# Attention kernel: the even transposes' bank is emptied between the exponentials of a pair's two heads

## The chip, the core and the metric

The kernel runs on one core of one Trainium2 chip. The metric is device time in microseconds (us) of one execution; the median of three runs of the kernel before is 1466.72 us (1466.05 to 1467.21). The engines are TensorE (PE in the rows, its weight loads PEld), VectorE (DVE), ScalarE (ACT), GpSimd (POOL) and SyncE (SP), which issues the loads and stores. Each engine works through its own queue in order, and they keep step by semaphores.

## What is computed

Sixteen blocks (batches) of 256 tokens by 256 features go through a first block of projections, then an attention with 16 heads of 64, then a layer of 8 experts. The change touches the attention alone. Of its reference:

```
shift = jax.nn.silu(t) @ W_ada.T + b_ada
h = _ln(x, ln1_g, ln1_b) + shift
qkv = (h @ Wqkv.T).reshape(b, n, 3, H, HD)
q = _ln(qkv[:, :, 0].transpose(0, 2, 1, 3), qn_g, qn_b)
k = _ln(qkv[:, :, 1].transpose(0, 2, 1, 3), kn_g, kn_b)
v = qkv[:, :, 2].transpose(0, 2, 1, 3)
scores = jnp.einsum('bhnd,bhmd->bhnm', q, k) / jnp.sqrt(jnp.float32(HD))
attn = jax.nn.softmax(scores, axis=-1)
o = jnp.einsum('bhnm,bhmd->bhnd', attn, v)
o = o.transpose(0, 2, 1, 3).reshape(b, n, H * HD)
x = x + o @ Wout.T
```

All matrix products but the values' and the transposes are made of three products of high and low parts.

## The kernel before

The attention runs over blocks t (written out one after the other, -2 to 17, of which 0 to 15 exist), and in each over pairs s = 0 to 7 of two heads, called the first and the second head (side 0 and 1). While block t's scores run, block t + 1's q, k and v are made ready, and the layer norm of block t + 2. Every engine has a function step(t, odd) in which the order of its queue is written by hand.

TensorE in pair s: the scores of both heads (scores, line 1103, into banks 3 and 4, one for each head); the transposes of the previous pair's probabilities (line 1115, banks 5 and 6); the fill of slot 2s, which I call the even one (four transposes into bank 0, called tr); the chunks of products for q, k, v of the next block (line 147, banks 1 and 2); in pairs 2 and 3 the output projection; the fill of slot 2s + 1, the odd one, again into bank 0; and in every second pair the value products of two pairs (line 1130). A table names what stands in the slots: x2 in slot 1, the layer norm's h in 2 (line 1192), the gates' products in 3 (line 1206), and eight transposes of q and k in slots 5 and 7 to 13 (line 1196). The even slots in use are thus 2, 8, 10 and 12: pairs 1, 4, 5 and 6. Before a fill, tr_free waits until ScalarE has emptied bank 0 of the one before:

```
TR_FILLS = [("x2", 0, 1), ("h", 0, 2), ("gates", 0, 3), ("qk", 0, 5)] + [("qk", j, 6 + j) for j in range(1, 8)]
```

ScalarE in pair s: the odd bank of the pair before (empty, line 1282 for q and k, with the norm's scale and bias); the values' high part (o_h, line 1328); two exponentials for each head (exps, line 1258), which wait for the row minima that VectorE takes of the scores (shift, line 1483); the copy of the transposed probabilities out of bank 5 (pT, line 1340); the high parts of q and k that are due (high_parts, line 1315); the even bank (empty; in pair 1 line 1276); and the copies of the chunks (lines 1302, 1304, 1309). VectorE takes the reciprocals of the sums (share_p, line 1489), GpSimd multiplies the probabilities with them (line 1382), and only then may TensorE transpose them in the next pair. GpSimd also scales q and k (line 1370) and makes low parts (lines 1376, 1408); the one of line 1408, rowsT_l, waits for VectorE's cast of line 1537 and is needed by the first chunk of pair 6. In block 14 the last fill of q and k is moved from slot 13 to 14 (LAST_NEAR, LATE_FILL), and block 15 has no next block to prepare.

Of the kernel before, what the change touches and what calls it, by code (L numbers as in the profile page):

```python
# [40 lines left out]
def live(b):  # L41

    return not isinstance(b, int) or 0 <= b < NB
# [824 lines left out]
PAIRS = H // 2  # L868
# [25 lines left out]
LAST_NEAR = NB - 2, 6  # L894
# [37 lines left out]
def attention(nc, exponent, weights, rows_of, banks, ident, x1_rows, hbias, cols, x2_rows, logit, out, a, halves, sbuf, sems):  # L932
# [4 lines left out]
    s = ExitStack()  # L937
    with s:
# [29 lines left out]
        def first(b):  # L968

            return isinstance(b, int) and b == 0  # L970
# [77 lines left out]
        with nc.Block() as block:  # L1048
# [200 lines left out]

            @block.scalar  # L1250
            def _(act):
                def exps(t, s):
                    for side in range(2):
                        at = s % 2 * 2 + side
                        wait(act, lowest, H, t, 2 * s + side + 1)
                        wait(act, pT_done, H, t, 2 * s + side - 3)
                        for n in range(TT):
                            last = nc.scalar.activation(prob[at][:, n, :], score_bank[side][:, n * T:(n + 1) * T], ACT.Exp,  # L1258
                                                        bias=shift[:, at, n:n + 1], scale=-1.0, accum_out=denom[:, at, n:n + 1])
                        last.then_inc(exped, 1)  # L1260

                def seeds(b, n):
                    wait(act, rooted, 2 * TT, b, 2 * n + 1)
                    nc.scalar.activation(logs[:, :], ssq[:, n, :], ACT.Ln).then_inc(seeded, 1)
                    wait(act, seeded, 2 * TT, b, 2 * n + 1)
                    wait(act, normed, 8, b - 1, (n + 1) * QKC)
                    nc.scalar.activation(rq[:, n, :], logs[:, :], ACT.Exp, scale=-0.5).then_inc(seeded, 1)

                def empty(b, name, j, its):
                    if name is None or not live(b) or name == "h" and first(b):  # L1270
                        return
                    if name == "h":
                        wait(act, tr_h, 1, b, 1)
                        wait(act, a_lo, 1, b - 1, 1)
                        for k in range(KT):
                            last = nc.scalar.activation(aT[:, k, :], tr[:, k * T:(k + 1) * T], ACT.Identity,
                                                        bias=hbias[:, k, bass.ds(b, 1)], scale=cols[:, LN1_G + k:LN1_G + k + 1])
                        last.then_inc(out_h, 1)
                    if name == "qk":
                        wait(act, tr_qk, 8, b, j + 1)  # L1280
                        g = QN_G if QK_ORDER[j] % QKC < 2 else KN_G
                        nc.scalar.activation(raw_block(j), tr[:, :].rearrange("p (m n) -> p m n", m=4), ACT.Identity,  # L1282
                                             bias=cols[:, g + 1:g + 2], scale=cols[:, g:g + 1]).then_inc(out_qk, 1)
                    if name == "x2":
                        wait(act, tr_x2, 1, b, 1)
                        nc.scalar.activation(x2T[:, :, :].rearrange("p k n -> p (k n)"), fill_bank(b)[:, :], ACT.Copy).then_inc(out_x2, 1)
                    if name == "gates":
                        wait(act, tr_gates, 1, b, 1)
                        nc.scalar.activation(logit[:, bass.ds(b * TT, TT), :], fill_bank(b)[:, 0:TT * E].rearrange("p (n e) -> p n e", n=TT), ACT.Copy).then_inc(out_gates, 1)

                def projected(b, n):
                    wait(act, tr_proj, TT, b, n + 1)
                    wait(act, tr_gates, 1, b - 1, 1)
                    nc.scalar.activation(proj[:, n, :], proj_bank(b, n)[:, 0:D], ACT.Copy).then_inc(out_proj, 1)

                def chunk(b, j, odd):
                    n, c = CHUNKS[j]
                    wait(act, chunk_done, 12, b, j + 1)
                    if c < QKC:
                        e = n * QKC + c  # L1300
                        wait(act, qk_lo, 8, b - 1, QK_ORDER.index(e) + 1)
                        nc.scalar.activation(raw[:, e, :], chunk_bank[j % 2][:, :], ACT.Copy)  # L1302
                        wait(act, summed, 8, b, e - 1)
                        nc.scalar.activation(raw_sq[e % 2][:, :], chunk_bank[j % 2][:, :], ACT.Square).then_inc(chunk_out, 1)  # L1304
                    else:
                        wait(act, pv_done, PAIRS, b - 2, PAIRS)
                        if isinstance(b, int) and b == 1:
                            act.wait_ge(wo_lo, FIRST_LO + 4)
                        nc.scalar.activation(v[1 - odd][:, n, (c - QKC) * 512:(c - QKC + 1) * 512], chunk_bank[j % 2][:, :], ACT.Copy).then_inc(chunk_out, 1)

                def high_parts(t, s, js, odd):
                    for j in js:
                        if live(t + 1) and HIGH_PAIR[j] == s:
                            wait(act, out_qk, 8, t + 1, j + 1)
                            nc.scalar.activation(block_of((qT_h, kT_h), j, 1 - odd), raw_block(j), ACT.Copy).then_inc(qk_hi, 1)

                def step(t, odd):
                    for s in range(PAIRS):
                        if not closing(t) and not closing(t - 1):
                            if s - 1 in PROJ_PAIRS and live(t - 1):  # L1320
                                projected(t - 1, PROJ_PAIRS.index(s - 1))
                            empty(*fill_at(t, 2 * s - 1), 1 - odd)
                        for b, q, its, n in taken_at(t, s, odd):
                            if live(b):
                                wait(act, pv_done, PAIRS, b, q + n)
                                if q in (0, 2):
                                    wait(act, tr_proj, TT, b - (2 if q == 0 else 1), TT)
                                nc.scalar.activation(o_part(o_h, q, its, n), result_of(b, q, n), ACT.Copy).then_inc(o_hi, n)
                        if closing(t) or closing(t - 1):
                            empty(*fill_at(t, 2 * s - 1), 1 - odd)  # L1330
                        for n in range(TT):
                            if live(t + 1) and s == SEED_PAIR[n]:
                                seeds(t + 1, n)
                        if live(t):
                            exps(t, s)
                        b, q, _ = pair_at(t, s, 1, odd)
                        if live(b):
                            wait(act, pT_done, H, b, 2 * q + 1)
                            wait(act, pv_done, PAIRS, b, q - 1)
                            nc.scalar.activation(pT[q % 2 * 2][:, :, :].rearrange("p m n -> p (m n)"), pT_bank[0][:, :], ACT.Copy).then_inc(pT_act, 1)  # L1340
                        late = t == LAST_NEAR[0] and s == PAIRS - 1
                        high_parts(t, s, range(7 if late else 8), odd)
                        empty(*fill_at(t, 2 * s), 1 - odd)
                        if late:
                            high_parts(t, s, (7,), odd)
                        for c, j in chunks_at(t, s):
                            if live(c):
                                chunk(c, j, odd)
                        if closing(t) and s in PROJ_PAIRS:
                            projected(t - 1, PROJ_PAIRS.index(s))  # L1350
                        for q in range(4):
                            if t == -1 and s == WOUT_HIGH_PAIR[q]:
                                nc.scalar.activation(flat(wo_h[:, :, :])[:, q * 512:(q + 1) * 512], flat(o_raw)[:, q * 512:(q + 1) * 512], ACT.Copy).then_inc(wo_hi, 1)
                        if live(t) and s == PIECE_PAIRS[0]:
                            wait(act, ew_piece, 32, t, 16)
                            wait(act, ew_stored, 32, t - 1, 32)
                            nc.scalar.activation(ew_h[:, :], ew_raw[:, :], ACT.Copy).then_inc(ew_piece, 8)
                steps(step)

            @block.gpsimd  # L1360
# [768 lines left out]
```

## Time and profile before

| | us |
|---|---|
| median of three runs | 1466.72 |
| lowest, highest | 1466.05, 1467.21 |
| the profiled execution | 1464.1 |
| its span | 1462.3 |
| TensorE busy (weight loads) | 1376.4 (1178.4) |
| ScalarE busy | 1038.9 |
| VectorE busy | 960.8 |
| GpSimd busy | 913.1 |

The attention's blocks stand between about 365 and 1190 us of the span. In a row of the timeline stand the start, the duration, the engine, the line, the operation, what it writes from what, and, where the engine was idle before it, how long and for whom. Ends of matrix products are modelled, so that the starts are the safer times. Where a row merges several instructions (x4), the duration is that of all.

### The profile page before, as it was taken

How to read it: one execution, taken by the hardware profiler on the slowest of the kernel's cores; microseconds unless marked ns; L12 is line 12 of the kernel's file. 1: busy time of each engine (PE TensorE's matmuls, PEld its weight loads, DVE VectorE, ACT ScalarE, POOL GpSimd, SP SyncE). 2: the span in 40 equal slices, each digit the busy share in tenths (PEclk: the TensorE clock that was granted, in tenths of full speed). 3: DMA queues.
4: the chain of work that ended last, by engine and by line, in shares of the span. 5: the costliest groups of instructions: out<-in, count | busy, mean ns of one | idle time of the engine just before them, and what ended most of it. 6: DMA issues, size and time to landing. Idle time of an engine off the chain costs nothing. (4 is left out here: it accounts for less than half of the span.)

```text
span 1462.3 us, 30429 instructions
## 1 busy us (share of the span) xinstructions
PE 1376.4 (94%) x10795; PEld 1178.4 (81%) x10795; DVE 960.8 (66%) x2191; ACT 1038.9 (71%) x2703; POOL 913.1 (62%) x855
## 2 busy tenths in 40 slices
PE   7899999998899999999999999999999889899997
PEld 5799999996677787787787777787778678889896
DVE  5877767645666566567666667667656568678763
ACT  5566666547888888888888888878888742466662
POOL 2676676543767867776776776876786730364633
PEclk9899999999999999999999999999999999999999
DMA  5432222110100110110110010010011028144622
GB/s 156 132 106 73 66 68 72 48 38 21 37 29 9 51 44 9 52 44 9 51 52 22 31 51 23 31 51 33 20 44 38 23 71 332 35 111 122 168 34 29
DMA packets 61638, 89.04 MB, mean 61 GB/s; under 512 B 6144, under 2 KB 50992, under 8 KB 58800
## 3 DMA queue, kind: packets, MB, share of 16 engines
q1 hardware_dynamic: 53232, 75.82, 16.0%
q0 software_dynamic: 6144, 8.39, 3.5%
q10 hardware_dynamic: 2112, 2.88, 0.6%
q8 instruction: 87, 1.43, 0.4%
q14 instruction: 63, 0.52, 0.1%
HBM read 61.90 MB, written 25.18 MB: 60 GB/s over the span
## 5 line engine op out<-in xcount | busy, mean ns | idle before, releaser
L1382 POOL TENSOR_TENSOR prob<-prob,share_p 128x512 f32<-128x512 f32 x256 | 271.5, 1067 | 229.3 <-DVE share_p L1489 228.7
L1483 DVE TENSOR_REDUCE shift<-bank 128x2 f32<-128x512 f32 x256 | 164.6, 684 | 251.3 <-PE bank L1103 251.1
L1258 ACT ACTIVATE prob<-bank,shift 128x256 f32<-128x256 f32 x512 | 235.7, 474 | 87.0 <-DVE shift L1483 86.9
L147 PE MATMUL bank<-wqkv_h,rowsT_h 128*128 128x512 f32 x384 | 159.0, 414 | 2.8 <-PEq L311 1.7
L147 PE MATMUL bank<-wqkv_h,rowsT_l 128*128 128x512 f32 x384 | 150.9, 393 | 0.0
L147 PE MATMUL bank<-wqkv_l,rowsT_h 128*128 128x512 f32 x384 | 150.8, 393 | 0.0
L1115 PE MATMUL bank<-ident,prob 128*128 128x128 f32 x1024 | 142.5, 281 | 1.3 <-POOL prob L1382 1.3
L1370 POOL TENSOR_TENSOR landing<-landing,rq 128x512 f32<-128x512 f32 x128 | 132.0, 1052 | 8.4 <-DVE rq L1437 8.4
L1130 PE MATMUL bank<-pT,landing 128*64 128x256 f32 x1024 | 126.2, 386 | 1.2 <-ACT pT L1340 1.2
L1115 PEld LDWEIGHTS bank<-ident,prob 128*128 128x128 f32 x1024 | 109.3, 141 | 21.7 <-POOL prob L1382 4.2
L1196 PE MATMUL bank<-ident,landing 128*128 128x128 f32 x512 | 79.2, 278 | 34.4 <-ACT landing L1282 31.9
L640 POOL TENSOR_TENSOR hid_l<-hid,hid_h 128x512 fp32r<-128x512 f32 x64 | 86.2, 1356 | 30.7 <-ACT hid_h L536 30.0
L1258 ACT ACTIVATION_READ_ACCUMULATOR prob<-bank,shift 128x1 f32 x512 | 104.7, 205 | 0.0
L1282 ACT ACTIVATE landing<-bank,cols 128x512 f32<-128x512 f32 x128 | 102.9, 804 | 2.2 <-PE bank L1196 0.6
L532 ACT ACTIVATE hid<-bank,cols 128x256 f32<-128x256 f32 x128 | 53.3, 470 | 68.2 <-PE bank L147 68.2
L1196 PEld LDWEIGHTS bank<-ident,landing 128*128 128x128 f32 x512 | 58.1, 142 | 53.5 <-issue 47.5
L1130 PEld LDWEIGHTS bank<-pT,landing 128*64 128x64 f32 x1024 | 67.2, 136 | 40.4 <-issue 9.3
L1103 PE MATMUL bank<-kT_h,qT_h 64*128 64x256 f32 x512 | 85.7, 330 | 3.1 <-ACT prob L1258 3.1
L1302 ACT ACTIVATE landing<-bank 128x512 f32<-128x512 f32 x128 | 80.4, 628 | 10.2 <-PE bank L147 10.2
L1514 DVE COPY pT<-bank 128x512 f32<-128x512 f32 x128 | 87.1, 680 | 0.2 <-PE bank L1115 0.2
L1479 DVE TENSOR_REDUCE ssq<-raw_sq 128x8 f32<-128x512 f32 x128 | 85.8, 672 | 1.3 <-ACT raw_sq L1304 0.7
L147 PEld LDWEIGHTS bank<-wqkv_h,rowsT_h 128*128 128x128 f32 x384 | 72.8, 190 | 16.3 <-issue 2.4
(324 smaller groups left out, 4528.2 us busy)
## 6 DMA issues: line engine op xcount, KB each, us to landing
landing<-in_fc1s SPq DMA_DIRECT2D x6, 1024.0 KB, 4.9
landing<-in_fc2s SPq DMA_DIRECT2D x6, 1024.0 KB, 5.0
rows<-in_x SPq DMA_DIRECT2D x16, 256.0 KB, 3.0
xT<-in_xT SPq DMA_DIRECT2D x16, 256.0 KB, 2.7
x_again<-in_x SPq DMA_DIRECT2D x16, 256.0 KB, 2.7
x_rows<-x SPq DMA_DIRECT2D x16, 256.0 KB, 3.2
rows<-x_rows SPq DMA_DIRECT2D x16, 256.0 KB, 3.1
x<-x_rows SPq DMA_DIRECT2D x16, 256.0 KB, 2.8
```

Source lines behind the costliest of these rows:

```text
L147: last = nc.tensor.matmul(out, a, b, start=(n == 0), stop=(n == 3 * len(ks) - 1))
L640: nc.gpsimd.tensor_tensor(hid_l[:, 2 * g:2 * g + 2, :], hid[:, 2 * g:2 * g + 2, :], hid_h[:, 2 * g:2 * g + 2, :].bitcast(F32), ALU.subtrac ...
L1115: last = nc.tensor.transpose(pT_bank[side][:, m * T + n * P:m * T + (n + 1) * P], prob[q % 2 * 2 + side][:, n, m * P:(m + 1) * P], ident[: ...
L1130: last = nc.tensor.matmul(values_bank(b, q)[side * HD:(side + 1) * HD, :], v[its][:, m, h * HD:(h + 1) * HD], pT[q % 2 * 2 + side][:, m, : ...
L1196: last = nc.tensor.transpose(tr[:, m * P:(m + 1) * P], raw_block(j)[:, m, :], ident[:, :])
L1258: last = nc.scalar.activation(prob[at][:, n, :], score_bank[side][:, n * T:(n + 1) * T], ACT.Exp, bias=shift[:, at, n:n + 1], scale=-1.0, ...
L1282: nc.scalar.activation(raw_block(j), tr[:, :].rearrange("p (m n) -> p m n", m=4), ACT.Identity, bias=cols[:, g + 1:g + 2], scale=cols[:, g ...
L1370: nc.gpsimd.tensor_tensor(part, part, rq[:, n, c * 8:(c + 1) * 8].unsqueeze(2).to_broadcast([P, 8, HD]), ALU.mult).then_inc(normed, 1)
L1382: nc.gpsimd.tensor_tensor(prob[at][:, :, :], prob[at][:, :, :], share[:, at, :].unsqueeze(2).to_broadcast([P, TT, T]), ALU.mult).then_inc( ...
L1479: nc.vector.tensor_reduce(ssq[:, n, c * 8:(c + 1) * 8], raw_sq[c % 2][:, :].rearrange("p (h d) -> p h d", h=8), AX, ALU.add).then_inc(summ ...
L1483: nc.vector.tensor_reduce(shift[:, s % 2 * 2 + side, :], score_bank[side][:, :].rearrange("p (n m) -> p n m", n=TT), AX, ALU.min).then_inc ...
L1514: nc.vector.tensor_copy(pT[q % 2 * 2 + 1][:, :, :].rearrange("p m n -> p (m n)"), pT_bank[1][:, :]).then_inc(pT_dve, 1)
```

## The change

ScalarE's step is written in another order. exps gets a list of sides, and is called once for the first head and once for the second; between the two calls stands the emptying of the even bank, which before came behind the copy of pT and the high parts. In pair 7 of block 14 (late) it stays where it was. No other engine's code is touched, and no instruction is added or left out.

```
-                def exps(t, s):
-                    for side in range(2):
+                def exps(t, s, sides):
+                    for side in sides:
...
+                        late = t == LAST_NEAR[0] and s == PAIRS - 1
                         if live(t):
-                            exps(t, s)
+                            exps(t, s, (0,))
+                        if not late:
+                            empty(*fill_at(t, 2 * s), 1 - odd)
+                        if live(t):
+                            exps(t, s, (1,))
...
-                        late = t == LAST_NEAR[0] and s == PAIRS - 1
                         high_parts(t, s, range(7 if late else 8), odd)
-                        empty(*fill_at(t, 2 * s), 1 - odd)
                         if late:
+                            empty(*fill_at(t, 2 * s), 1 - odd)
                             high_parts(t, s, (7,), odd)
```

ScalarE's queue in pairs 5 and 6 of a block, before (L1282 is written once for the even bank, once for the odd one; L1258 x4 are the exponentials of both heads):

```order
L1328 ACTIVATE o_h<-bank 128x512
L1258 ACTIVATE prob,denom<-bank,shift 128x256 x4
L1340 ACTIVATE pT<-bank 128x512
L1315 ACTIVATE kT_h<-landing 128x4x128 x2
L1282 ACTIVATE landing<-bank,cols 128x512
L1309 ACTIVATE landing<-bank 128x512 x2
L1282 ACTIVATE landing<-bank,cols 128x512
L1258 ACTIVATE prob,denom<-bank,shift 128x256 x4
L1340 ACTIVATE pT<-bank 128x512
L1315 ACTIVATE qT_h<-landing 128x4x128
L1315 ACTIVATE kT_h<-landing 128x4x128
L1282 ACTIVATE landing<-bank,cols 128x512
```

And now (line 1340 has become 1345):

```order
L1328 ACTIVATE o_h<-bank 128x512
L1258 ACTIVATE prob,denom<-bank,shift 128x256 x2
L1282 ACTIVATE landing<-bank,cols 128x512
L1258 ACTIVATE prob,denom<-bank,shift 128x256 x2
L1345 ACTIVATE pT<-bank 128x512
L1315 ACTIVATE kT_h<-landing 128x4x128 x2
L1309 ACTIVATE landing<-bank 128x512 x2
L1282 ACTIVATE landing<-bank,cols 128x512
L1258 ACTIVATE prob,denom<-bank,shift 128x256 x2
L1282 ACTIVATE landing<-bank,cols 128x512
L1258 ACTIVATE prob,denom<-bank,shift 128x256 x2
L1345 ACTIVATE pT<-bank 128x512
```

The even bank's L1282 has moved ahead of two exponentials, the copy of pT and the high parts; the odd bank's stands where it stood.

ScalarE's queue in pair 1 of a block, before, where the even bank holds the layer norm's transposes (L1276):

```order
L1267 ACTIVATE rq<-logs 128x32
L1258 ACTIVATE prob,denom<-bank,shift 128x256 x4
L1340 ACTIVATE pT<-bank 128x512
L1276 ACTIVATE rowsT<-bank,hbias,cols 128x256 x2
L1302 ACTIVATE landing<-bank 128x512
```

And now:

```order
L1267 ACTIVATE rq<-logs 128x32
L1258 ACTIVATE prob,denom<-bank,shift 128x256 x2
L1276 ACTIVATE rowsT<-bank,hbias,cols 128x256 x2
L1258 ACTIVATE prob,denom<-bank,shift 128x256 x2
L1345 ACTIVATE pT<-bank 128x512
L1302 ACTIVATE landing<-bank 128x512
```

Both instructions of L1276 have moved ahead of the second head's exponentials and the copy of pT.

## Rows read from the trace of the kernel before

**Rows 1.** Attention: stretch, its us, busy us of PE PEld DVE ACT POOL, clock, DMA.
```profile
365.00:1190.00 825.00, 790.48 (x6087) 632.38 (x6087) 529.38 (x1170) 686.84 (x1917) 594.56 (x553) 1.00 0.11 34
```

**Rows 2.** Line 1196, what its engine sat idle for: us, times.
```profile
  ACT landing L1282: 31.9, 46
```

**Rows 3.** TensorE, pair 5 of block 6: start, us, engine, line, operation.
```profile
709.97 0.39 PE L1103 MATMUL bank<-kT_h,qT_h 64*128 64x256 f32 x2
...
711.81 0.60 PE L1196 MATMUL bank<-ident,landing 128*128 128x128 f32 x4
...
714.75 0.39 PE L147 MATMUL bank<-wqkv_h,rowsT_l 128*128 128x512 f32 x1
715.98 0.63 PE L1196 MATMUL bank<-ident,landing 128*128 128x128 f32 x4 [0.83 <-ACT landing L1282]
716.53 0.38 PE L1103 MATMUL bank<-kT_h,qT_h 64*128 64x256 f32 x2
```

**Rows 4.** ScalarE, pairs 5 to 7 of block 6, in order of time.
```profile
711.71 0.47 ACT L1258 ACTIVATE prob<-bank,shift 128x256 f32<-128x256 f32 x1 [0.97 <-DVE shift L1483]
...
713.52 0.61 ACT L1340 ACTIVATE pT<-bank 128x512 f32<-128x512 f32 x1
...
715.04 0.80 ACT L1282 ACTIVATE landing<-bank,cols 128x512 f32<-128x512 f32 x1
715.70 1.11 ACT L1309 ACTIVATE landing<-bank 128x512 f32<-128x512 f32 x2
716.65 0.82 ACT L1282 ACTIVATE landing<-bank,cols 128x512 f32<-128x512 f32 x1
718.27 0.48 ACT L1258 ACTIVATE prob<-bank,shift 128x256 f32<-128x256 f32 x1 [0.80 <-DVE shift L1483]
...
724.17 0.84 ACT L1282 ACTIVATE landing<-bank,cols 128x512 f32<-128x512 f32 x1
...
726.71 0.47 ACT L1258 ACTIVATE prob<-bank,shift 128x256 f32<-128x256 f32 x1 [0.96 <-DVE shift L1483]
```

**Rows 5.** TensorE, pair 4 of block 0: odd transposes that do not wait.
```profile
389.17 0.40 PE L147 MATMUL bank<-wqkv_h,rowsT_l 128*128 128x512 f32 x1
389.40 0.60 PE L1196 MATMUL bank<-ident,landing 128*128 128x128 f32 x4
```

**Rows 6.** TensorE, pairs 4, 6 and 1 (the block after).
```profile
706.83 0.39 PE L147 MATMUL bank<-wqkv_h,rowsT_l 128*128 128x512 f32 x1
707.53 0.63 PE L1196 MATMUL bank<-ident,landing 128*128 128x128 f32 x4 [0.32 <-ACT landing L1282]
...
721.37 0.39 PE L147 MATMUL bank<-wqkv_h,rowsT_l 128*128 128x512 f32 x1
722.54 0.63 PE L1196 MATMUL bank<-ident,landing 128*128 128x128 f32 x4 [0.79 <-ACT landing L1282]
723.10 1.95 PE L1130 MATMUL bank<-pT,landing 128*64 128x256 f32 x16
...
741.59 0.39 PE L147 MATMUL bank<-wqkv_h,rowsT_l 128*128 128x512 f32 x1
742.01 1.03 PE L1206 MATMUL bank<-wgate,proj 128*128 128x8 f32 x8
```

**Rows 7.** ScalarE, pair 1: the even bank with the layer norm.
```profile
740.83 1.04 ACT L1276 ACTIVATE rowsT<-bank,hbias,cols 128x256 f32<-128x256 f32 x2
```

**Rows 8.** VectorE, GpSimd and TensorE's weight loads, pairs 5 and 6.
```profile
714.23 0.17 DVE L1489 RECIPROCAL share_p<-denom 128x2 f32<-128x2 f32 x1
...
715.94 1.28 POOL L1408 TENSOR_TENSOR rowsT_l<-rowsT,rowsT_h 128x512 fp32r<-128x512 f32 x1 [0.43 <-DVE rowsT_h L1537]
...
718.70 0.19 PEld L147 LDWEIGHTS bank<-wqkv_h,rowsT_h 128*128 128x128 f32 x1
```

**Rows 9.** Block 14, pair 6: ScalarE's copy of pT, TensorE's values.
```profile
1145.65 0.61 ACT L1340 ACTIVATE pT<-bank 128x512 f32<-128x512 f32 x1
...
1146.31 1.08 PE L1130 MATMUL bank<-pT,landing 128*64 128x256 f32 x8 [0.76 <-ACT pT L1340]
```

## The prediction, made before the changed kernel was run

> **What bounds the kernel now.** I read the views in this order: busy time by stretch, what TensorE's groups wait for, then the timelines of TensorE and ScalarE through one block of the attention. The 16 blocks of the attention take 825 us of the 1462.3 us span and are nearly alike. In them [rows 1] TensorE is busy for 790.48 us, ScalarE for 686.84, GpSimd for 594.56, VectorE for 529.38, at a granted clock of 1.00. So TensorE sets the time, and what can be won is its idle time. The groups' view says where most of that is: the transposes of line 1196 sat idle 31.9 us in 46 waits for ScalarE's line 1282 [rows 2]. TensorE writes four transposes into bank 0, ScalarE copies the bank out with scale and bias, and TensorE may not write the next four before that.
>
> Counted along TensorE's timeline, three of the 46 lie in each of blocks 1 to 13 (pairs 4, 5, 6), two each in blocks 0 (pairs 5, 6) and 14 (pairs 4, 5), and three ahead of block 0, where ScalarE has no exponentials. It is always the odd transposes (the pair's second set) that wait for the bank of the even ones.
>
> Pair 5 of block 6 shows it. TensorE starts the scores at 709.97, the even transposes at 711.81 (over by 712.41), its last product of the pair at 714.75, and the odd transposes only at 715.98 [rows 3]. ScalarE does not empty the bank until 715.04 [rows 4]: ahead of it in its queue stand all four exponentials, the copy of pT and the two high parts of kT. The bank's contents have lain ready for 2.6 us by then. The wait is thus one of order, not of work.
>
> **What a stall costs.** Where nothing waits, the transposes start 0.23 us after the product before them (389.17 and 389.40) [rows 5]. In pair 5 they start 1.23 after it: 1.00 lost. Pair 6: 721.37 to 722.54, 1.17, so 0.94 lost. Pair 4: 706.83 to 707.53, 0.70, so 0.47 lost. The same thing happens in pair 1, where the even bank holds the layer norm's transposes (emptied by line 1276) and the gates' products follow: 741.59 to 742.01, 0.42, so 0.19 lost [rows 6]. Per block 2.60 us. The idle column says less (0.83 in pair 5 where I count 1.00), because it starts at the modelled end of the product before, which overlaps the next start. The Trainium skill warns of this (Perfetto Trace Analysis, Identifying the Most-Contended Engine): matmul busy time is a poor measure of headroom, since matmuls are pipelined. The trace agrees: 31.9 us of idle over 46 waits is 0.69 each, while starts against starts give 0.80 for the mean of pairs 4 to 6. By the idle column alone the 43 waits in the blocks would be worth 43 x 0.69 = 30 us instead of the sum below.
>
> **The change, part by part.** No instruction is added or removed. In pairs 1, 4, 5 and 6 ScalarE's emptying of the even bank moves ahead of the second head's two exponentials (block 14's pair 7 keeps the old order).
>
> (1) When does it now run? The four exponentials issue from 711.71 to 713.52 [rows 4], so the first head's two are through half-way, at 712.62: 2.65 after the scores' start. The even transposes are over at 2.44. So ScalarE does not wait for them, by 0.2 us. The emptying takes the slot from 2.65 and ends 0.80 later at 3.45; the odd transposes want the bank at 5.01 (714.75 + 0.23). They have 1.5 us to spare, and the whole stall goes. In pair 1 the two halves of line 1276 (1.04 us) [rows 7] end at 3.69, the gates want the bank at 5.0: it goes too.
>
> (2) What is later? The second head's exponentials, the copy of pT and the high parts, by the slot of the emptying: 715.70 - 715.04 = 0.66 us (0.90 in pair 1). From the slot in which the bank was emptied before, ScalarE's queue is as it was, since the same work stands ahead.
> - The copy of pT ended at 713.52 + 0.61, 4.16 after the scores; now 4.82. The value products that need it (pairs 4 and 6) start 0.56 after the odd transposes [rows 6], so now at 5.6: 0.8 to spare.
> - VectorE's reciprocal for the second head stood at 714.23 (4.26) because VectorE was late with other work; the exponentials are now over at 4.33, so it and the split of rowsT behind it slip by 0.10. GpSimd's low part of rowsT ran from 715.94 to 717.22, now 0.10 later; TensorE's first weight load that needs it stood at 718.70 and comes 1.00 sooner, at 717.70 [rows 8]. 0.4 us to spare, the narrowest place that I find.
> - The next pair's scores need the exponentials' end; in pair 5 they start at 5.56 instead of 6.56, against 4.33 for the exponentials.
>
> (3) Is ScalarE on time for the next pair? In pair 5 it starts its last piece, the odd emptying, at 716.65 and is free at 717.31; the exponentials of pair 6 stood at 718.27 after 0.80 of idle for the row minima [rows 4]. TensorE being 1.00 sooner, they are wanted at 717.27. ScalarE is 0.04 late, for the first time the one that is waited for, but the exponentials have 0.8 us in front of the next thing on TensorE. For pair 7 it starts the odd emptying at 724.17, which with the copy of the value products (o_h, 0.48) behind it keeps it until 724.17 + 0.66 + 0.48 = 725.31; the exponentials stood at 726.71 [rows 4] and are wanted 0.94 sooner, at 725.77, so 0.46 is left. From pair 7 on, each engine stands to TensorE as before. So the block runs 2.60 us shorter, with ScalarE 87% busy (686.84 of 825 less the 36 of the sum below) instead of 83.
>
> (4) Where it costs. In block 14's pair 6 TensorE has no chunk of products and no odd transposes; the values wait there for the copy of pT (0.76 idle, the copy starts at 1145.65) [rows 9]. The copy comes 0.66 later, and this time TensorE pays it.
>
> **Sum.** Pair 4: 14 blocks x 0.47 = 6.6. Pair 5: 15 x 1.00 = 15.0. Pair 6: 14 x 0.94 = 13.2. Pair 1: 12 (blocks 2 to 13, which have both layer norm and gates) x 0.19 = 2.3. Less 0.66 in block 14. Ahead of block 0 the emptying already waits for TensorE, and I take 0. Together 36.4 us. The profiled execution took 1464.1 us (span 1462.3), so 1427.7; the median of the runs is 1466.7, so **1430.3 us**.
>
> **Rivals.**
> (A) The stall goes, but a new wait takes a part. The candidates are the 0.4 us in front of GpSimd's low part and ScalarE's 0.04 us in pair 6, at 2.6 us less per block. For it: several margins shrink at once in pairs 5 to 7, and I replayed them from one block's durations. Against it: each of them is still positive, and after pair 7 there is slack again. If one pair per block gave back its 1.00 us, 14 us would be lost: 1444.
> (B) Nothing changes, because the odd transposes would next wait for GpSimd's normalised blocks (line 1370), which share their line with the bank's wait. Against it: the waits' view names ScalarE 46 times. 1466.7.
> (C) Slower. ScalarE now waits for a bank that TensorE fills only after the previous pair's transposes of prob, and these wait for GpSimd's division, which waits for the very exponentials that are put back. If the delay of the second head reached TensorE in all four pairs, as it does in block 14's pair 6, it would cost 3 x 0.66 + 0.90 = 2.88 a block against 2.60 won: 14 x 0.28 = 4 us more, 1471. It decides once the copy of pT or the division has under 0.66 us in hand; I find 0.8 after the delay at the copy, and more at the division.
> (D) The clock falls as TensorE has fewer gaps. Against it: it is 96% busy now and is granted 1.00 throughout [rows 1]. I give it nothing of its own.
>
> **Chances and range.** Forecast 0.78 (its own range 1426 to 1437, the far end by the idle column), A 0.14, B 0.03, C 0.05. A measurement of this kernel tells about 0.2% (3 us) from no change: faster 0.92, same 0.03, slower 0.05. Range 1426 to 1441: below, 4 us for stalls that I under-counted (each stalled set also runs 0.03 us longer) and blocks whose pair 6 lost a little more than block 6's; above, it takes in most of A.
>
> **What would show it.** In the profile after: line 1196's idle for line 1282 down from 31.9 us to the few of the prologue (under 5); the span from one block's scores to the next down by 2.6; exponentials in pair 6 starting about 0.04 us behind the minima; the wait of line 1130 for pT in block 14 at 1.4 instead of 0.76. Wrong would be: line 1282 idle for tens of us (the bank not full at 2.44), a wait of line 147 for rowsT_l in pair 6 (A), or line 1115 waiting for prob in steady blocks (C).

## The result, and the profile after

The changed kernel takes 1431.62 us (median of four runs, 1430.79 to 1432.67), the kernel before 1466.38 (four runs, 1464.22 to 1467.21). The ratio is 0.9766, with a 95% interval of 0.9749 to 0.9782: faster by 34.8 us. The forecast was 1430.3. The profiled execution took 1431.61 us, its span 1429.8.

The attention's blocks, by stretch (us, then busy us of PE, PEld, DVE, ACT, POOL, the granted clock, DMA share, GB/s); it answers to [rows 1]:

```profile
365.00:1160.00 795.00, 787.51 (x6115) 639.57 (x6113) 532.35 (x1175) 685.64 (x1920) 595.17 (x553) 1.00 0.11 36
```

TensorE's busy time has hardly moved (790.48 to 787.51), ScalarE's neither; a stretch that is 30 us shorter holds the same work. ScalarE is busy 685.64 of 795 us, 86%. The transposes of line 1196, and what their engine sat idle for (us, times); the row on line 1282 answers to [rows 2], 31.9 us in 46 waits:

```profile
  POOL landing L1374: 8.2, 7
  issue: 7.1, 17
  ACT landing L1282: 3.7, 3
```

The three waits left for line 1282 are those ahead of block 0. "issue" is idle time without a named releaser. The same view of the kernel before has under it

```profile
  issue: 47.5, 45
```

43 of these 45 stand at the weight loads of the very 43 odd sets whose matrix products waited for line 1282 (1.23 in pair 5, where 1.00 was lost), so it is the same loss, read in TensorE's other queue. The 17 that are left become important below.

TensorE through pair 5 of block 6, from its scores to the next pair's, and on through pair 6 (start, us, engine, line, operation):

```profile
695.62 0.39 PE L1103 MATMUL bank<-kT_h,qT_h 64*128 64x256 f32 x2
...
697.46 0.60 PE L1196 MATMUL bank<-ident,landing 128*128 128x128 f32 x4
...
700.40 0.40 PE L147 MATMUL bank<-wqkv_h,rowsT_l 128*128 128x512 f32 x1
700.64 0.60 PE L1196 MATMUL bank<-ident,landing 128*128 128x128 f32 x4
701.17 0.38 PE L1103 MATMUL bank<-kT_h,qT_h 64*128 64x256 f32 x2
...
703.27 0.63 PE L1196 MATMUL bank<-ident,landing 128*128 128x128 f32 x4
...
706.24 0.40 PE L147 MATMUL bank<-wqkv_h,rowsT_l 128*128 128x512 f32 x1
706.48 0.60 PE L1196 MATMUL bank<-ident,landing 128*128 128x128 f32 x4
```

The odd transposes start 0.24 after the last product (700.40 to 700.64), where it was 1.23 in [rows 3]; in pair 6 also 0.24 (706.24 to 706.48), where it was 1.17 in [rows 6]. Both stalls are gone. Something else is there too: in pair 5 the *even* transposes start 1.84 after the scores (697.46 - 695.62), in pair 6 2.10 after them (703.27 - 701.17). Their weight load stands in the queue PEld as

```profile
703.24 0.42 PEld L1196 LDWEIGHTS bank<-ident,landing 128*128 128x128 f32 x4 [0.31 <-issue]
```

so that it had waited 0.31 us, with no releaser named.

ScalarE beside it; these rows answer to [rows 4]:

```profile
698.27 0.78 ACT L1282 ACTIVATE landing<-bank,cols 128x512 f32<-128x512 f32 x1
698.93 0.48 ACT L1258 ACTIVATE prob<-bank,shift 128x256 f32<-128x256 f32 x1
...
699.83 0.61 ACT L1345 ACTIVATE pT<-bank 128x512 f32<-128x512 f32 x1
...
702.30 0.82 ACT L1282 ACTIVATE landing<-bank,cols 128x512 f32<-128x512 f32 x1
702.96 0.52 ACT L1258 ACTIVATE prob<-bank,shift 128x256 f32<-128x256 f32 x1
...
703.93 0.78 ACT L1282 ACTIVATE landing<-bank,cols 128x512 f32<-128x512 f32 x1
```

In pair 5 the even bank is emptied from 2.65 after the scores (698.27 - 695.62), as forecast, and its slot is 0.66 (to 698.93). The odd bank of pair 5 is emptied from 702.30, which is 1.13 after the scores of pair 6; before, it was 0.12 after them (716.65 to 716.53, [rows 3, 4]). ScalarE's queue stands where it stood, and TensorE has moved up by 1.00.

The length of each pair, from the start of its scores to the next scores, the same in blocks 2 to 13 within 0.04 us:

| pair | before | after | forecast of the difference | measured |
|---|---|---|---|---|
| 0, 2, 3, 7 together | 24.18 | 24.21 | 0 | +0.03 |
| 1 | 6.17 | 5.90 | -0.19 | -0.27 |
| 4 | 7.93 | 7.43 | -0.47 | -0.50 |
| 5 | 6.56 | 5.55 | -1.00 | -1.01 |
| 6 | 8.44 | 7.72 | -0.94 | -0.72 |
| the block | 53.28 | 50.80 | -2.60 | -2.48 |
| 6 of block 14 | 5.22 | 6.01 | +0.66 | +0.79 |

The span is 32.5 us shorter, and it adds up so: pair 4, 14 x 0.50 = 7.0; pair 5, 15 x 1.01 = 15.1; pair 6, 14 x 0.72 = 10.1; pair 1, 12 x 0.27 = 3.2; together 35.4. Against it: 0.8 in block 14's pair 6; 0.65 in block 15, whose pairs 0 and 1 now take 5.55 + 3.93 instead of 4.36 + 4.47; 0.4 ahead of block 0, which starts at 365.31 instead of 364.94 (364.3 to 366.3 in the traces below); and 1.0 behind the attention (from the scores of block 15's last pair to the end, 279.1 instead of 278.1). That last part runs the same instructions and differs from run to run (278.2 to 279.4 in the traces below), so I read nothing into either. The profiled execution of before lay 2.3 us under its median, which is why the medians differ by 34.8 and the spans by 32.5.

### The profile page after: what moved, and what is told of

It is laid out like the page before. It is cut to its first block and busy times, and to the rows that moved or that the text cites. A ratio compares the mean times of both kernels' runs of the same rounds, so it can differ in the third digit from the quotient of the medians.

```text
span 1429.8 us, 30429 instructions
## 1 busy us (share of the span) xinstructions
PE 1370.5 (96%) x10795; PEld 1183.3 (83%) x10795; DVE 960.7 (67%) x2191; ACT 1035.9 (72%) x2703; POOL 911.5 (64%) x855
## 5 line engine op out<-in xcount | busy, mean ns | idle before, releaser
L1258 ACT ACTIVATE prob<-bank,shift 128x256 f32<-128x256 f32 x512 | 237.8, 479 | 64.3 <-DVE shift L1487 64.2
L1258 ACT ACTIVATION_READ_ACCUMULATOR prob<-bank,shift 128x1 f32 x512 | 107.5, 210 | 0.0
L1282 ACT ACTIVATE landing<-bank,cols 128x512 f32<-128x512 f32 x128 | 101.9, 796 | 4.9 <-PE bank L1196 3.3
L147 PEld LDWEIGHTS bank<-wqkv_h,rowsT_l 128*128 128x128 f32 x384 | 72.5, 189 | 15.8
```

What stands on the lines that cost most here:

```text
L147: last = nc.tensor.matmul(out, a, b, start=(n == 0), stop=(n == 3 * len(ks) - 1))
```

## The experiments

The kernels below are compared in two ways. By time, each beside nine runs of the kernel before on the same chip (median 1466.15 for the first four, 1466.69 for the others). And by the lengths of the pairs in one profiled execution, which two profiled executions of the changed kernel give alike to 0.04 us in blocks 1 to 14; this tells differences of 0.1 us in a pair apart, which the times can't.

### Pair 5 alone

```
-                        if not late:
+                        moved = s == 5
+                        if moved:
                             empty(*fill_at(t, 2 * s), 1 - odd)
...
-                        if late:
+                        if not moved:
                             empty(*fill_at(t, 2 * s), 1 - odd)
+                        if late:
```

> Of the change only pair 5 is kept: the even bank is emptied between the two heads' exponentials there, and in the old place (behind the copy of pT and the high parts) in all other pairs. My theory: each pair's stall is a term of its own, so pair 5 is 5.55 us long as in the changed kernel instead of 6.56, and pairs 4 and 1 are as before (7.93, 6.17). Pair 6 keeps its old stall and is about 8.49, 0.05 more than before, since ScalarE reaches it 0.05 late; the new 0.26 us wait of the even transposes there hides in the old stall. 15 x 1.01 - 14 x 0.05 = 14.4 us less than before: about 1452. Rival (the won time is handed on to the next wait, ScalarE being the bound): pair 6 grows by most of what pair 5 wins, under 7 us won, 1460 or more.

Measured: 1450.18 us (1449.95 to 1451.93), ratio 0.9897 (0.9882 to 0.9912). Pair 5 takes 5.55, as in the full change; pairs 4 and 1 are as before (7.92, 6.17), and pair 6 is 0.10 *longer* than before, 8.54 against 8.44. TensorE in pair 6 of block 6:

```profile
709.21 0.39 PE L1103 MATMUL bank<-kT_h,qT_h 64*128 64x256 f32 x2
...
711.31 0.63 PE L1196 MATMUL bank<-ident,landing 128*128 128x128 f32 x4
...
715.32 0.63 PE L1196 MATMUL bank<-ident,landing 128*128 128x128 f32 x4 [0.65 <-ACT landing L1282]
```

The even transposes start 2.10 after the scores, as in the full change, though pair 6's own order is the old one. So it is the shorter pair 5 that makes them late, and not pair 6's own change. Here the odd set waits for ScalarE in any case, so the 0.26 us cost nothing; its wait is only shorter for them (0.65 instead of the 0.79 of [rows 6]). The 0.10 comes from ScalarE's emptying of the even bank, first in this version, then in the kernel before:

```profile
714.32 0.86 ACT L1282 ACTIVATE landing<-bank,cols 128x512 f32<-128x512 f32 x1
```

```profile
721.60 0.80 ACT L1282 ACTIVATE landing<-bank,cols 128x512 f32<-128x512 f32 x1
```

It starts 5.11 after the scores instead of 5.07 (709.21 and 716.53), since ScalarE reaches pair 6 late, and lasts 0.06 longer. The forecast had the first part and not the second.

### The odd bank of pair 5 emptied one instruction earlier

In the changed kernel's pair 5 the odd bank is full at 701.24 (700.64 + 0.60), and ScalarE starts the two copies of line 1309 at 701.34, with the emptying behind them. In this version the emptying stands between those two instead of behind both.

```
-                            empty(*fill_at(t, 2 * s - 1), 1 - odd)
+                            if s != 6:
+                                empty(*fill_at(t, 2 * s - 1), 1 - odd)
...
-                        for c, j in chunks_at(t, s):
+                        for n, (c, j) in enumerate(chunks_at(t, s)):
                             if live(c):
                                 chunk(c, j, odd)
+                            if n == 0 and s == 5:
+                                empty(*fill_at(t, 2 * s + 1), 1 - odd)
```

> The changed kernel, and besides ScalarE empties pair 5's odd bank between the copies of that pair's two chunks instead of behind them. Theory: what pair 6 won less than I forecast (8.44 to 7.72, where 7.47 was due) is a new wait of its even transposes, which start 2.10 us after the scores instead of 1.84 because the odd bank of pair 5 is not empty yet. ScalarE's emptying comes one copy (0.48 us) sooner, and this wait goes: pair 6 7.46 long, 14 x 0.26 = 3.6 us less than the changed kernel, 1428.0. Rival (the even transposes of pair 6 are late for another reason, or the second chunk's copy, now 0.66 later, holds TensorE up): pair 6 stays at 7.72, or its first or second chunk waits, 1431.6 or more.

Measured: 1427.98 us (1426.61 to 1430.92), ratio 0.9747 (0.9733 to 0.9760). Pair 6 takes 7.47 instead of 7.72; no other pair of a steady block differs. TensorE in pair 6 of block 6:

```profile
699.48 0.39 PE L1103 MATMUL bank<-kT_h,qT_h 64*128 64x256 f32 x2
...
701.31 0.60 PE L1196 MATMUL bank<-ident,landing 128*128 128x128 f32 x4
```

ScalarE at the same place:

```profile
699.65 0.62 ACT L1309 ACTIVATE landing<-bank 128x512 f32<-128x512 f32 x1
700.13 0.81 ACT L1282 ACTIVATE landing<-bank,cols 128x512 f32<-128x512 f32 x1
```

The emptying starts 0.65 after the scores instead of 1.13, and the even transposes are back at 1.83 after them. This shows the cause of the 0.25 us. It also shows where the view hid it: what line 1196's engine sat idle for now reads

```profile
  ACT landing L1282: 3.7, 3
  issue: 2.4, 2
```

Fifteen waits have left the row "issue" (17 to 2, and 7.1 to 2.4 us): 4.7 us, 0.31 each, as many as there are pairs 6 in blocks 0 to 14. They were waits for ScalarE that carried no name of a releaser, since they were seen at the weight load ahead of the transposes.

### Block 14 as before

```
-                        if not late:
+                        old = t == LAST_NEAR[0] and s >= PAIRS - 2
+                        if not old:
                             empty(*fill_at(t, 2 * s), 1 - odd)
...
-                        if late:
+                        if old:
                             empty(*fill_at(t, 2 * s), 1 - odd)
+                        if late:
```

> The changed kernel, but block 14's pair 6 keeps the old order (its pair 7 does already). Theory: the length of that pair falls from 6.01 to about 5.27 us, since the copy of pT, for which TensorE waits there, no longer stands behind the emptying: 0.7 us. The changed kernel's TensorE clock was granted at 0.5 (1.2 GHz) from 1118.9 to 1122.3 in block 15, right behind that longer wait (1.25 us idle) and another of 1.37; before the change, with 0.76 and 1.37, it was not. If the one brought the other, the lower clock goes too and block 15's pairs 0 and 1 together take 8.83 instead of 9.48: 1.4 us less than the changed kernel in all, 1430.2. Rival (the clock falls there by chance or by something else): it stays or comes and goes, 0.7 us less, 1430.9.

Measured: 1431.74 us (1430.13 to 1432.63), ratio 0.9765 (0.9751 to 0.9778). Pair 6 of block 14 falls from 6.01 to 5.33, by 0.68, the slot of the emptying. The 0.11 that stays over the 5.22 of before is ScalarE's, which TensorE waits for here: the exponentials start 1.79 after the scores instead of 1.74, and the copy of pT lasts 0.67 instead of the 0.61 of [rows 9]. The late odd bank of pair 5 has no part in it: the version with both remedies, below, empties that bank earlier, and this pair takes 5.34 there. TensorE's values in that pair, in the changed kernel; the second row answers to [rows 9], where it waited 0.76:

```profile
1109.82 1.08 PE L1130 MATMUL bank<-pT,landing 128*64 128x256 f32 x8
1112.15 1.08 PE L1130 MATMUL bank<-pT,landing 128*64 128x256 f32 x8 [1.25 <-ACT pT L1345]
```

The same in this version:

```profile
1111.97 1.08 PE L1130 MATMUL bank<-pT,landing 128*64 128x256 f32 x8
1113.63 1.08 PE L1130 MATMUL bank<-pT,landing 128*64 128x256 f32 x8 [0.57 <-ACT pT L1346]
```

The second question was block 15. In the changed kernel TensorE's granted clock there is low for a while, which it was not before. Busy time by stretch, over 6 us from block 15's start and over the low part of them, in the changed kernel (the granted clock is the third number from the right):

```profile
1117.00:1123.00 6.00, 5.78 (x40) 3.73 (x42) 3.77 (x11) 5.25 (x15) 5.59 (x6) 0.72 0.01 3
...
1119.00:1122.00 3.00, 3.00 (x14) 1.53 (x13) 1.84 (x5) 2.81 (x11) 3.00 (x3) 0.50 0.00 0
```

In this version, over the low part:

```profile
1121.00:1123.50 2.50, 2.50 (x12) 1.31 (x12) 1.33 (x4) 2.50 (x10) 2.50 (x3) 0.50 0.00 0
```

In the kernel before:

```profile
1151.00:1157.00 6.00, 5.32 (x48) 3.73 (x48) 4.44 (x12) 5.48 (x15) 5.59 (x6) 1.00 0.01 3
```

I had thought that the longer wait in block 14 brings the clock down. Here the wait is short again, and the clock falls all the same, to 0.50 of full speed (the 1.2 GHz level). That theory fell. In this trace there is a second such stretch in block 0's pair 4, which takes 9.91 us with it and 8.51 without:

```profile
387.00:390.00 3.00, 2.92 (x11) 2.73 (x12) 1.19 (x3) 1.70 (x6) 3.00 (x4) 0.50 1.02 338
```

So the 0.68 won in block 14 is not to be seen in the time, and it is less than two runs of one kernel differ by.

### Behind the copy of pT

```
-                        if not late:
-                            empty(*fill_at(t, 2 * s), 1 - odd)
                         if live(t):
                             exps(t, s, (1,))
...
+                        if not late:
+                            empty(*fill_at(t, 2 * s), 1 - odd)
                         high_parts(t, s, range(7 if late else 8), odd)
```

> The even bank is emptied right behind the copy of pT, ahead of the high parts, instead of between the two heads. Theory: the emptying only has to be over before the odd transposes want the bank, 5.01 us after the scores; there it ends at 4.83 in pairs 4 to 6, so these pairs are as in the changed kernel (7.43, 5.55, 7.72) within 0.05. In pair 1, which has no high parts, this is the old place: 6.17 again instead of 5.90, 3.2 us more. Block 14's pair 6 gets its 0.7 us back, and block 15 its clock: 1.4 less. In sum 1.8 us more than the changed kernel, 1433.4. Rival (the bank must be free early, or the delay of the second head's exponentials costs something everywhere): pairs 4 to 6 differ from the changed kernel by 0.1 us or more each, up if the first, down if the second.

Measured: 1432.73 us (1431.27 to 1434.99), ratio 0.9775 (0.9762 to 0.9789), so by time not to be told from the changed kernel. By pairs: pair 4 takes 7.42, pair 5 5.54, pair 6 7.77, and block 14's pair 6 5.35. The stalls of pairs 4 to 6 need the emptying ahead of the high parts only, not between the heads. Pair 1 takes 6.18, as before; there both instructions end too late for the gates' products. TensorE in this version:

```profile
675.40 0.39 PE L147 MATMUL bank<-wqkv_h,rowsT_l 128*128 128x512 f32 x1
675.84 1.03 PE L1206 MATMUL bank<-wgate,proj 128*128 128x8 f32 x8
676.80 0.38 PE L1103 MATMUL bank<-kT_h,qT_h 64*128 64x256 f32 x2
```

In the changed kernel:

```profile
674.73 0.40 PE L147 MATMUL bank<-wqkv_h,rowsT_l 128*128 128x512 f32 x1
674.96 0.95 PE L1206 MATMUL bank<-wgate,proj 128*128 128x8 f32 x8
675.85 0.39 PE L1103 MATMUL bank<-kT_h,qT_h 64*128 64x256 f32 x2
```

0.44 against 0.23 from the last product to the gates' products, and these last 0.96 against 0.89 to the next scores. So a set that had to wait also runs 0.07 longer, which is why pair 1 won 0.27 and not 0.19.

### How much delay the second head bears: pairs 4 and 5

The high parts of q and k, too, are put ahead of the second head's exponentials, one instruction of ScalarE in pair 4 (0.52 us more delay), two in pair 5 (1.04). In this version in pairs 4 and 5:

```
+                        ahead = s in (4, 5)
+                        if ahead:
+                            high_parts(t, s, range(8), odd)
                         if live(t):
                             exps(t, s, (1,))
...
-                        high_parts(t, s, range(7 if late else 8), odd)
+                        if not ahead:
+                            high_parts(t, s, range(7 if late else 8), odd)
```

> The changed kernel, and in pairs 4 and 5 ScalarE also makes the high parts of q and k (0.52 us in pair 4, two of them, 1.04 us, in pair 5) ahead of the second head's exponentials. It prices the margins of the forecast. Theory: in pair 4 the copy of pT ends 5.34 us after the scores, the values want it at 5.6, so pair 4 stays at 7.43. In pair 5 the second head's reciprocal comes 1.04 later, behind it VectorE's cast of rowsT and GpSimd's rowsT_l, which I reckoned to be 0.4 us early for the first chunk of pair 6 (a little more now that the even transposes start 0.26 late): TensorE waits about 0.6 us there, pair 5 stays at 5.55 and pair 6 grows from 7.72 to about 8.3. 14 x 0.6 = 8 us over the changed kernel, 1440. Rival (the second head has time, nothing on TensorE hangs on it): pair 6 stays at 7.72, 1431.6.

Measured: 1439.35 us (1436.95 to 1440.00), ratio 0.9807 (0.9792 to 0.9822). Pairs 4 and 5 stay at 7.43 and 5.55; pair 6 goes to 8.25 (7.85 in block 13, where rowsT_l is started 1.22 after the scores and not 1.63; why it is earlier there is open). GpSimd at the end of pair 5 and in pair 6 of block 6 (scores of pair 6 at 706.47):

```profile
706.63 1.04 POOL L1390 TENSOR_TENSOR prob<-prob,share_p 128x512 f32<-128x512 f32 x1 [1.45 <-DVE share_p L1497]
708.10 1.27 POOL L1416 TENSOR_TENSOR rowsT_l<-rowsT,rowsT_h 128x512 fp32r<-128x512 f32 x1 [0.43 <-DVE rowsT_h L1545]
```

TensorE in pair 6:

```profile
709.47 0.47 PE L147 MATMUL bank<-wqkv_h,rowsT_h 128*128 128x512 f32 x1 [0.27 <-issue]
```

rowsT_l is split from 1.63 after the scores, where the changed kernel has it 0.59 after them (701.76), and the chunk starts 3.00 after them instead of 2.48. 1.04 of delay cost 0.53 (8.25 - 7.72), so the margin in front of it is 0.5 in the changed kernel. That is the narrow place that the prediction named. But its 0.4 was reckoned for a chunk that is not held up, and here the chunk stands 0.3 later, behind the late even transposes. GpSimd, and then TensorE's weight load that needs rowsT_l, in the version with the odd bank emptied earlier, where the transposes are on time (scores at 699.48):

```profile
700.07 1.28 POOL L1415 TENSOR_TENSOR rowsT_l<-rowsT,rowsT_h 128x512 fp32r<-128x512 f32 x1 [0.43 <-DVE rowsT_h L1544]
```

```profile
701.64 0.19 PEld L147 LDWEIGHTS bank<-wqkv_h,rowsT_h 128*128 128x128 f32 x1
```

rowsT_l is over 1.87 after the scores and the load starts at 2.16: 0.29 apart, read as the forecast read its 0.38. The steps from rowsT_l's end to the load take 0.07 when the load waits (2.90 to 2.97 after the scores in the version of this section), so about 0.2 is really to spare.

### How much delay the second head bears: pairs 4 and 6

```
+                        ahead = s in (4, 6)
```

with the rest as above.

> As the run before, but in pairs 4 and 6. Theory: pair 4 again stays at 7.43. In pair 6 the copy of pT moves from an end at about 4.95 us after the scores to 5.99; the values want it at 5.83: a wait of about 0.2, pair 6 about 7.93, and block 14's pair 6, where TensorE always waits for that copy, 1.04 longer (6.01 to 7.05). 14 x 0.2 + 1 = 4 us over the changed kernel, 1435.5. Rival (the 0.8 us in front of the values was a wrong reckoning): larger margin, pair 6 at 7.72, 1432.6; smaller, pair 4 longer as well.

Measured: 1432.31 us (1430.27 to 1435.63), ratio 0.9771 (0.9756 to 0.9786). Block 14's pair 6 takes 7.05, 1.04 more, just as expected. But pair 6 of the steady blocks takes 7.72, no longer than without the edit, where I had expected a loss of 0.2. ScalarE's copy of pT in pair 6 of block 6 (scores at 700.18):

```profile
705.57 0.60 ACT L1348 ACTIVATE pT<-bank 128x512 f32<-128x512 f32 x1
```

TensorE's values:

```profile
706.02 1.95 PE L1130 MATMUL bank<-pT,landing 128*64 128x256 f32 x16
```

The values start at 706.02 while the copy runs until 706.17. They are two sets of eight, and only the second set needs the pair's own copy; block 14's rows above show the two apart. The first set lasts about 1 us (half of 1.95), so the copy had that much more time than the 0.8 us that I had given it.

### The changed kernel once more

> The changed kernel once more, unaltered. It asks whether the stretch of lower clock in block 15 belongs to this kernel. Theory after the runs so far: it does not, it comes and goes from run to run, since it was there with the shorter wait too and absent with the longer one; so the pairs of blocks 1 to 14 repeat to 0.03 us, and a lower clock stands somewhere else or in another number of stretches. Rival (it belongs to the order): at the same place again, block 15's pair 0 at 5.5.

One execution: 1431.2 us. The pairs are as in the first trace, within 0.04 us from block 1 to block 14, and block 15's clock is low again:

```profile
1117.00:1123.00 6.00, 5.79 (x44) 3.73 (x40) 3.49 (x10) 5.26 (x15) 5.63 (x6) 0.72 0.01 3
```

So my theory missed and the rival came out. Two of two speaks for something of this program and against chance, yet it doesn't follow the waits. The version with high parts ahead in pairs 4 and 5 has the changed kernel's waits, 1.25 us in block 14 and 1.38 at block 15's start (1.25 and 1.37 in the first trace), and is granted full clock in block 15; TensorE in block 14 there, and the busy time from block 15's start:

```profile
1121.33 1.08 PE L1130 MATMUL bank<-pT,landing 128*64 128x256 f32 x8 [1.25 <-ACT pT L1348]
```

```profile
1126.00:1132.00 6.00, 5.31 (x48) 3.73 (x48) 4.43 (x12) 5.50 (x16) 5.59 (x6) 1.00 0.01 3
```

So is the version with the longest wait there (2.29 us, pairs 4 and 6); TensorE there:

```profile
1112.34 1.08 PE L1130 MATMUL bank<-pT,landing 128*64 128x256 f32 x8 [2.29 <-ACT pT L1348]
```

Its busy time by stretch:

```profile
1117.00:1123.00 6.00, 5.29 (x48) 3.73 (x48) 4.43 (x12) 5.51 (x16) 5.59 (x6) 1.00 0.01 3
```

### Both remedies together

The odd bank one instruction earlier, and block 14 in the old order (the two diffs above in one kernel).

> The two repairs together: pair 5's odd bank emptied between its chunk copies, and block 14's pair 6 in the old order. Theory: 3.6 + 0.7 us less than the changed kernel, 1427.3; pair 6 at 7.47 in blocks 0 to 13, 5.27 in block 14. The 0.7 alone cannot be told from 1428.0 by the time, only by the trace. Rival (the two get in each other's way): 1428 or more with pair 6 of block 14 above 5.4.

Measured: 1427.93 us (1427.68 to 1428.88), ratio 0.9734 (0.9720 to 0.9747). Pair 6 takes 7.47, block 14's pair 6 5.34, and block 15 is granted full clock. ScalarE's copy of pT in block 14's pair 6, for which TensorE waits:

```profile
1109.36 0.68 ACT L1347 ACTIVATE pT<-bank 128x512 f32<-128x512 f32 x1
```

It starts 3.60 after the scores (1105.77), 0.05 later than before, and lasts 0.68 instead of 0.61: the same 0.11 to 0.12 as with the late bank, so these come from ScalarE and not from the bank. Block 0's pair 4 lost 1.3 in its profiled execution to a low clock like the one above (9.81 instead of 8.52). This version beats the changed kernel by about 4 us; from the version with only the odd bank's move it can't be told.

## Why the prediction was right, and where its steps were off

**What bounds the kernel, and the stall: right.** The wait was one of order. No wait of the odd sets for line 1282 is left in any block (the 15 of the even sets in pair 6 come under part 3), pairs 4 and 5 won what starts against starts had given (0.50 and 1.01 for 0.47 and 1.00), and pair 5 alone shortened the span by 14.1 us (1462.3 to 1448.2), where 15 x 1.01 less 15 x 0.10 in pair 6 gives 13.7.

**How to count a wait: right.** The idle column fell by 28.2 us (31.9 to 3.7) while pairs 4, 5 and 6, whose waits it counts, became 32.2 us shorter, and would have become 35.7 shorter without the new wait of part (3) (32.2 + 14 x 0.25). The idle column is a part of the loss only, here as in the forecast's warning. Its "30 us by the idle column alone" was itself a little high: the three waits ahead of block 0 have 3.7 of the 31.9, and the 43 in the blocks 28.2.

**Part (3), is ScalarE on time for the next pair: the step that failed.** The prediction followed ScalarE into pair 6 and found it 0.04 late for the exponentials. That was right: they start 1.79 after the scores instead of 1.74 (702.96 to 701.17, and 718.27 to 716.53 in [rows 3, 4]). But it asked only who waits for the exponentials, and not who waits for the last thing that ScalarE does ahead of them: the emptying of the odd bank. Bank 0 is waited for both ways. The odd set waits for the even one to be emptied, and the next pair's even set for the odd one. TensorE came 1.00 sooner, ScalarE's odd emptying did not, and a gap that had covered it was gone: 14 x 0.22 = 3.1 us of the forecast 13.2 for pair 6. Pair 5 alone showed that it comes from pair 5 being shorter, and moving the odd bank's emptying by one instruction took it away. This is rival A's mechanism (a new wait takes a part) at a place that rival A did not name, and at a fifth of its price.

**Pair 1: mis-sized.** 0.27 instead of 0.19, 1.0 us over 12 blocks, because a set that waited also runs slower (0.07 here, 0.03 for the transposes); the prediction had it as a remark on the range and not in the sum.

**Part (2), the margins: both mis-sized, without harm.** The place in front of rowsT_l was named rightly. It has 0.5 in the changed kernel, but only because the chunk behind it is late; where the transposes are on time it is 0.29, not 0.38, of which about 0.2 is to spare. The forecast let rowsT_l slip by 0.10; it starts 6.14 after pair 5's scores instead of 5.97, 0.17 later. The 0.8 at the copy of pT is the margin of the first of two sets of values, which doesn't need that copy; for the second set it is about 1 more. Rival C (1471) turned on this copy or the division having under 0.66 in hand. The copy in pair 6 and the division in pair 5 were each put back by another 1.04, and neither made TensorE wait in the steady blocks.

**Part (4), block 14: right in kind, 0.13 short.** 0.79 for 0.66. The copy of pT, for which TensorE waits, starts 4.34 after the scores (1107.16) instead of 3.55:

```profile
1111.50 0.60 ACT L1345 ACTIVATE pT<-bank 128x512 f32<-128x512 f32 x1
```

0.68 is the slot, 0.05 is ScalarE being late for the exponentials, and 0.07 its wait for the even transposes, which are late here too (the emptying starts at 2.76 instead of 2.69). Part (3) had found the lateness, but the sum did not charge it in the one pair where TensorE waits for ScalarE. With the odd bank emptied earlier the 0.07 goes, but the copy then lasts 0.68, and the pair takes 5.99, so the earlier bank wins nothing here. Why the copy runs longer where ScalarE had no idle time before it is open. The wait itself was forecast at 1.4 and reads 1.25, because the first set of values starts 2.66 after the scores instead of 2.36 (1109.82 to 1107.16), behind the late even transposes; the length of the pair is the safer measure.

**The clock: not foreseen.** Rival D looked for a falling clock in the steady blocks, where it stayed at 1.00. It fell at one place, in block 15, which cost 0.65. What brings it about there is open. It was seen in both profiled executions of the changed kernel and in the one with block 14 as before, and in none of the kernel before or of the six other versions. The length of block 14's wait doesn't decide it: it stands with the low clock at 0.57 and at 1.25 (block 14 as before, changed kernel) and without it at 0.57, 1.25 and 2.29 (pair 5 alone, pairs 4 and 5, pairs 4 and 6), the wait at block 15's start being 1.37 or 1.38 in all of them.

**The total.** In the profiled execution's own terms the forecast was 1427.7, and it took 1431.6: 3.1 from pair 6's even set, 1.0 from the end, 0.65 from block 15, 0.4 from the start and 0.1 from block 14, less 1.0 and 0.4 that pairs 1 and 4 gave over it. Against the medians it is 1.3 off, since the forecast added the 2.6 by which the kernel before's median lay above its profiled execution, and the changed kernel's median lies on its own. Some of the closeness of the medians is thus luck.

## What to carry to other kernels

When one buffer is filled and emptied by turns, look at both waits: after the one is removed, the producer arrives earlier at the other, and an engine whose queue did not move then stands later beside it by just what was won (1.13 us after the scores instead of 0.12, of which 0.26 became a wait). Count a stall from start to start, and look at the weight loads' "issue" rows as well, since a wait for a buffer can be recorded there without its releaser's name. Before pricing the delay of a step that was put back, ask which of its consumer's instructions really needs it: of sixteen value products, only the last eight did.

## What the runs showed that I had not expected

The granted clock was 0.50 for about 3 us at places where TensorE was busy, and not at the same places in other traces. Ahead of the low clock in block 15 of the changed kernel TensorE had waited 1.25 us in block 14 and 1.37 us for ScalarE's exponentials, and it was then busy for all of the 3 us at 0.50. In block 0 the low clock stood in three versions (block 14 as before, pairs 4 and 5, both remedies). One such stretch cost 0.65 us in block 15 and 1.3 to 1.4 us in block 0's pair 4. The same waits stand in traces without it: the version with high parts ahead in pairs 4 and 5 waited 1.25 and 1.38 us there and kept 1.00. What brings it about is open. In a comparison of versions a microsecond can come from this, and the lengths of the pairs in the trace tell it apart.
